# Two heads side by side in the rows of the matmul array, in the first attention of a four-layer model

## The reference, cut to what matters

```python
y = jnp.einsum('oc,bct->bto', W, x)            # Q, K, V: 16 heads of 16
att = jnp.einsum('bhqd,bhkd->bhqk', Q, K) * (1.0 / math.sqrt(Dh))
att = att + b[0]
m = mask[:, None, None, :]
att = att * m + (1.0 - m) * NEG_INF            # NEG_INF = -1e30
att = jax.nn.softmax(att, axis=-1)
y = jnp.einsum('bhqk,bhkd->bhqd', att, V)      # x = x + y, transposed back
```

## Time and profile before

| | us |
|---|---|
| median of 3 runs | 2042.97 (2039.57 to 2043.9) |
| the profiled execution's own time | 2042.31 |
| its span in the trace | 2040.5 |
| mean granted TensorE clock in it | 0.958 of full |
| both attentions with their preparations, to the end of the last scores stage | 0 to 1000 |
| second attention of the last item alone, recurrence, last layer | 1000 to 2040 |

### The profile page before, as it was taken

The page is one execution under the profiler, slowest core; times in us unless marked ns, Lnnn a source line. Parts: engine busy times, 40 slices in busy tenths (PEclk is TensorE's granted clock), DMA queues, the critical chain, the costliest instruction groups (busy, mean ns, idle before and its releaser), DMA issues. The chain is left out here.

```text
span 2040.5 us, 87545 instructions
## 1 busy us (share of the span) xinstructions
PE 1885.0 (92%) x33246; PEld 1408.9 (69%) x33246; DVE 1255.9 (62%) x5543; ACT 1095.2 (54%) x4105; POOL 380.2 (19%) x1398
## 2 busy tenths in 40 slices
PE   8887998999989999899887999999999999999996
PEld 4234454464644636446456999999999999999995
DVE  6545383654836447364333677777777777777767
ACT  0342736637356363654744466656666666666554
POOL 3000000000000000000000234343434333343335
PEclk7778999999999999999998999999999999999997
DMA  5122213223032230412223000000000000000002
GB/s 190 70 74 53 82 28 97 66 53 92 19 101 62 66 92 6 106 41 73 74 62 108 3 0 0 0 0 0 0 0 0 0 0 0 0 0 0 0 0 83
DMA packets 103527, 86.76 MB, mean 43 GB/s; under 512 B 15616, under 2 KB 90496, under 8 KB 103440
## 3 DMA queue, kind: packets, MB, share of 16 engines
q1 hardware_dynamic: 101392, 84.38, 14.4%
q10 hardware_dynamic: 1664, 1.18, 0.2%
q0 software_dynamic: 384, 0.01, 0.0%
HBM read 60.20 MB, written 21.00 MB: 40 GB/s over the span
## 5 line engine op out<-in xcount | busy, mean ns | idle before, releaser
L1255 PE MATMUL bank_pair_A<-moving,rep 128*128 128x16 f16 x8192 | 318.5, 170 | 2.5 <-ACT bank_pair_C L1346 1.4
L1255 PE MATMUL bank_pair_C<-moving,rep 128*128 128x16 f16 x8192 | 316.2, 169 | 0.0
L1255 PE MATMUL bank_pair_B<-moving,rep 128*128 128x16 f16 x8192 | 316.1, 169 | 0.0
L1255 PEld LDWEIGHTS bank_pair_A<-moving,rep 128*128 128x128 f16 x8192 | 274.7, 96 | 14.2 <-issue 4.0
L1355 ACT ACTIVATE r_gate<-r_pre 128x16 f32<-128x16 f32 x512 | 110.5, 216 | 286.5 <-DVE r_pre L1446 286.5
L1255 PEld LDWEIGHTS bank_pair_C<-moving,rep 128*128 128x128 f16 x8192 | 258.9, 96 | 0.0
L1255 PEld LDWEIGHTS bank_pair_B<-moving,rep 128*128 128x128 f16 x8192 | 258.9, 96 | 0.0
L1242 PE MATMUL bank_pair_D<-x_part,w_in 128*128 128x256 f16 x1536 | 198.6, 275 | 7.3 <-ACT gi_rz L1382 4.7
L1137 POOL TENSOR_TENSOR x<-x,w_in 128x512 f32<-128x512 f32 x8 | 10.2, 1272 | 960.5 <-DMA w_in<-w_in 960.5
L1446 DVE TENSOR_REDUCE r_pre<-bank_pair_A 128x16 f32<-128x32 f32 x512 | 98.1, 192 | 133.7 <-PE bank_pair_A L1255 133.7
L834 ACT ACTIVATE probs<-bank_pair_A 128x1024 f32<-128x1024 f32 x128 | 130.9, 1023 | 89.6 <-PE bank_pair_A L598 89.2
(11 more groups left out here) (262 smaller groups left out, 3786.0 us busy)
## 6 DMA issues: line engine op xcount, KB each, us to landing
rep<-parts SPq DMA_DIRECT2D x256, 64.0 KB
parts<-parts SPq DMA_DIRECT2D x48, 256.0 KB, 2.1
q_rep<-parts SPq DMA_DIRECT2D x32, 256.0 KB, 4.8
k_rep<-parts SPq DMA_DIRECT2D x64, 128.0 KB, 2.9
w_in<-in_x_dram SPq DMA_DIRECT2D x8, 512.0 KB, 4.0
x<-in_x_dram SPq DMA_DIRECT2D x8, 512.0 KB, 4.3
parts<-parts SPq DMA_DIRECT2D x32, 128.0 KB, 2.6
out_dram<-res SPq DMA_DIRECT2D x16, 256.0 KB, 2.0
```

The source lines that it names most:

```text
L1255: last = nc.tensor.matmul(ps[part][:, o:o + 2 * B], w[:, k, (first + c) * P:(first + c) * P + P], moving[j % 2][:, k, :, :].rearrange("p s ...
```

## The change

Two heads now stand in partitions 0 to 63 and 64 to 127 of `q_rep` and `k_rep`, and each matmul of the first attention has 64 rows; the two of a pair are issued one after the other, in different halves of the array's rows. The mask and bias partitions are gone: keys are centred by their masked mean (so that a masked key, now zero, has the score of the mean key), and mask and bias stand in the exponential's bias. The maximum is added by a second pair of matmuls of 64 rows. The functions keep their places in the order of steps.

```diff
             def load_rep(b, g):
...
-                sp.dma_start(k_rep[64:67, heads, :], mask_rows[b:b + 1, :, :].rearrange("o r t -> (o r) t").unsqueeze(1)
-                             .broadcast_to([3, 4, D])).then_inc(ld_rep[g], 16)
                 sp.wait_ge(st_parts, b * 64 + 64)
-                for rep0, rows in ((q_rep, ((0, 0), (0, 32), (1, 16), (1, 48))), (k_rep, ((2, 0), (2, 16), (3, 32), (3, 48)))):
-                    for n, row in rows:
-                        sp.dma_start(rep0[row:row + DH0, heads, :], parts0[n][heads, :, :].rearrange("h d t -> d h t")).then_inc(ld_rep[g], 16)
+                for s in range(2):
+                    heads, pairs = slice(4 * g + s, 4 * g + 4, 2), slice(2 * g, 2 * g + 2)
+                    for rep0, rows in ((q_rep, ((0, 0), (1, 16), (1, 32), (0, 48))), (k_rep, ((2, 0), (2, 16), (3, 32), (3, 48)))):
+                        for n, row in rows:
+                            row += s * P // 2
+                            sp.dma_start(rep0[row:row + DH0, pairs, :], parts0[n][heads, :, :].rearrange("h d t -> d h t")).then_inc(ld_rep[g], 16)
...
-                for qc in range(2):
-                    t0 = (2 * (u % 2) + qc) * P
-                    last = nc.tensor.matmul(pair[u % 2][:, qc, :], q_rep[0:96, u // 2, t0:t0 + P], k_rep[0:96, u // 2, :],
+                t0 = u % DC * P
+                for s, half in enumerate(HALF):
+                    last = nc.tensor.matmul(pair[u % 2][:, s, :], q_rep[half, u // DC, t0:t0 + P], k_rep[half, u // DC, :],
                                             start=True, stop=True)
...
-                for j in range(4):
-                    h = 4 * g + j
-                    last = nc.tensor.matmul(pair[u % 2][:, j // 2, (j % 2) * N:(j % 2) * N + N], k_rep[:, h, kc * P:kc * P + P],
-                                            q_rep[:, h, queries], start=(j % 2 == 0), stop=True, skip_group_check=True)
+                for s, half in enumerate(HALF):
+                    nc.tensor.matmul(pair[u % 2][:, s, :], k_rep[half, p, kc * P:kc * P + P], q_rep[half, p, :], start=True, stop=False)
+                for s, half in enumerate(HALF):
+                    last = nc.tensor.matmul(pair[u % 2][:, s, :], max_sel[half, :], max_rep[half, p, :], start=False, stop=True)
...
+                    nc.vector.scalar_tensor_tensor(out=kf[:, c, :], in0=k[:, c, :], scalar=1.0, in1=mask_bc[:, :], op0=ALU.mult,
+                                                   op1=ALU.mult, accum_out=key_sum[:, c:c + 1]).then_inc(k_sum, 1)
+                dve.wait_ge(k_sum, 3 * b + 2)
+                nc.vector.tensor_scalar(key_sum[:, :], key_sum[:, :], seen[:, 1, b:b + 1], None, ALU.mult).then_inc(k_sum, 1)
+                dve.wait_ge(k_sum, 3 * b + 3)
+                for c in range(NC):
+                    last = nc.vector.scalar_tensor_tensor(out=kf[:, c, :], in0=k[:, c, :], scalar=key_sum[:, c:c + 1], in1=mask_bc[:, :],
+                                                          op0=ALU.subtract, op1=ALU.mult)
```

More of the change, by code:

```diff
@@ L174, in attention @@
             cond_sb = mask_bc[0:B, :]
-            rows = y[0:B, :, :].rearrange("p a b -> p (a b)").bitcast(F16)[:, 0:3 * D].rearrange("p (r d) -> p r d", r=3)
             block = prep.enter_context(nc.Block())
@@ L250, in _ @@
                 last.then_inc(c_condt, 1)
+                pe.wait_ge(c_copied, 4)
+                for c in range(DC):
+                    last = nc.tensor.matmul(pC[:, 1, 0:B], ones32[:, 0:1].broadcast_to([P, P]), condT[:, c, :], start=(c == 0), stop=(c == DC - 1))
+                last.then_inc(c_count, 1)
         ld_x1, ld_mask, st_parts, ld_max = (sem(n) for n in ("ld_x1", "ld_mask", "st_parts", "ld_max"))
@@ L812, in k_part @@
                 act.wait_ge(kf_ok, b + 1)
-                nc.scalar.activation(k_hi[:, :, :], kf[:, :, :], ACT.Copy).then_inc(k_hi_ok, 1)
+                nc.scalar.activation(k_hi[:, :, :], kf[:, :, :], ACT.Copy, scale=QS).then_inc(k_hi_ok, 1)
             def v_part(b):
@@ L827, in max_rows @@
                 act.wait_ge(max_ok, b + 1)
-                act.dma_start(q_rep[96:97, :, :].rearrange("o h (c t) -> o (h c) t", c=DC), max_row[:, :]).then_inc(ld_max, 16)
+                for s in range(2):
+                    act.dma_start(max_rep[s * P // 2:s * P // 2 + 1, :, :].rearrange("o h (c t) -> o (h c) t", c=DC),
+                                  max_row[s * U0:s * U0 + U0, :]).then_inc(ld_max, 16)
             def exponent(b, u):
@@ L833, in exponent @@
                     act.wait_ge(pv_ps, b * W0 + (u // 2 - 1))
-                nc.scalar.activation(probs[u // 2 % 2][:, :, u % 2 * N:u % 2 * N + N],
-                                     pair[u % 2][:, :, :].rearrange("p a (b t) -> p (a b) t", b=2), ACT.Exp, scale=LOGIT0).then_inc(exp_ok, 1)
+                kc = u // 2 % DC
+                nc.scalar.activation(probs[u // 2 % 2][:, 2 * (u % 2):2 * (u % 2) + 2, :], pair[u % 2][:, :, :], ACT.Exp,
+                                     bias=mask_bias[:, kc, b:b + 1], scale=LOGIT0).then_inc(exp_ok, 1)
             def inverse(b, g):
@@ L977, in k_part @@
                 dve.wait_ge(k_hi_ok, b + 1)
-                nc.vector.tensor_tensor(k_lo[:, :, :], kf[:, :, :], k_hi[:, :, :], ALU.subtract).then_inc(k_lo_ok, 1)
+                nc.vector.scalar_tensor_tensor(out=k_lo[:, :, :], in0=kf[:, :, :], scalar=QS, in1=k_hi[:, :, :],
+                                               op0=ALU.mult, op1=ALU.subtract).then_inc(k_lo_ok, 1)
             def group_sums(b, g):
@@ L1120, in _ @@
         def _(pool):
-            pair_of_rows = float(np.array([ROW, ROW], np.float16).view(np.float32)[0])
             nc.gpsimd.memset(v_aug[:, :, :, DH0:], 1.0).then_inc(c_later, 1)
```

86 lines of the change are left out of this document (38 added, 48 removed).

## The result

| | median us (lowest to highest) | ratio to the kernel before, 95% interval |
|---|---|---|
| before | 2041.96 (2039.57 to 2043.90) | |
| changed | 2081.61 (2080.13 to 2082.90) | 1.0188 (1.0174 to 1.0202) |

The change makes the kernel 39.6 us slower; 15 were predicted. The span of the profiled execution grew from 2040.5 to 2078.0. I cut it at the first attention's exponentials: a scores stage reaches from the start of an item's first to the end of its last, a maxima stage from there to the next item's first. Both columns of the table are differences to the kernel before.

What follows compares the result with a forecast made beforehand. PE, busy 92% of the span, was taken as the bound. Scores stages +22.2, maxima stages -15.6 and start +8.3 gave +14.9 on 2042.3, that is 2057, forecast as 2058 us for the median; range 2028 to 2088 (80%).

Steps and rivals of the forecast that it cites:

- a pair costs 0.22 (512 columns) plus 0.007: First attention's matmuls: two in different row halves overlap as strips do, taking 0.22 us plus 0.007; without overlap 0.43.
- Price 0.097 at full clock: PE, each switch between full-array matmuls and matmuls of 64 rows: 0.097 us, as for strips; the other end is 0.
- 12 + 7 = 19 changes, 1.84 us: Scores stage: twelve q, k, v projection slots each add a mode change before, seven also one behind; 1.84 us, unhidden.
- The 0.41 for DVE: Second attention's maxima, eight slots: PE waits 0.41 us within each pair, hiding all but one mode change, leaving 0.4 us.
- 2.54 a stage: Scores stage of items 1 to 6, without the centred-key wait: units 0.2, mode changes 1.84, 0.4 and 0.1 us.
- The exponential keeps its shape, its bias costs nothing: First attention's exponential on ACT: same shape as before, and the added bias operand takes no time.
- Centred keys, 0.7: Scores stages of items 1 to 6: PE waits 0.7 us for `kf`, delayed by two more passes and one small step.
- Maxima stages: Half-row units shorten the stage by 2.1 us an item, six times -12.6; item 0 -3 (0 to -6); sum -15.6.
- Groups between `weigh1`: Maxima stage, four units between two `weigh1`, paced by DVE: -0.33 us a group, three groups -1.0.
- the gain of 3 that was predicted: Item 0's maxima stage, units in threes and part of it at half clock: -3 us (0 to -6).
- Start: Before the first exponential: later bias load +4.9, centred keys +1.6, 16 DMA issues +2.6, among others; +8.3 us.
- weights load in the open: Rival: the pair's second matmul starts one load (0.10 us) late, adding 25 to 50 us, 2080 to 2105; chance 11%.

## Why the prediction was wrong

The direction was right, and most of the working on mode and overlap too. The size failed, by 22.6 us of span: 10.2 in the scores stages, 8.0 in the maxima stages of items 1 to 6 and 5.9 in item 0's, less 0.9 at the start and 0.6 at the end. Two steps failed with their cause shown: the price of a change of mode left out the weight load behind it, and the exponential's bias was put at nothing. Item 0's maxima stage is a third, and its cause stays open.

- **"a pair costs 0.22 (512 columns) plus 0.007", "Price 0.097 at full clock": right.** The halves overlap, and a change costs 0.09 to 0.10. That strips of 32 and 8-row transposes speak for 64 rows, and 96 rows do not, held. The Trainium skill (TensorEngine Tiling (Array Packing), Key Properties) has a change of mode drain the engine, and these 0.09 to 0.10 agree with it. The load in the open comes on top.
- **Changes in the scores stage, "12 + 7 = 19 changes, 1.84 us": mis-sized.** The mechanism was right, the price of one was not: a slot behind a change pays for 0.10 of weight load too, and so each of the twelve slots costs that much more than I charged. With units and boundaries I had 2.54 a stage; 3.0 were measured, not 2.54 + 1.2. I take the rest to fall where PE waits anyway, which no run isolates. The 0.41 for DVE in this sum was also misread, as said above.
- **"The exponential keeps its shape, its bias costs nothing": this step failed.** It costs 0.09 each, 23 us of ACT time, of which 0.45 us a stage reached the end in items 1 to 6, and 1.3 in item 7, because a pair without slots now takes ACT as long as PE. That makes 5 us in all. Two rows of before gave the price, and I had not looked at them.
- **Centred keys, 0.7: 0.9 at full clock**, with 0.78 shown as PE's wait. The second pair of passes took 1.41 where 1.29 was reckoned, and the reads of the sums 0.08 each.
- **Maxima stages: mis-sized twice.** Groups between `weigh1` gave what was predicted; among f32 work the same weight load in the open took most of the rest (nine times 0.10), so 1.0 a stage came in place of 2.1. That is 6.6 of the 8.0 us; the other 1.4 is clock, which was below 1.00 in four of the six stages here and in three of six before. In item 0 the stage grew by 2.9 against -3. PE had less to do there than before (53.92 against 57.50 us busy), but more of it at half clock: 0.76 against 0.79 granted, and 0.81 with maxima of all rows, whose stage was 79.7 with 55.90 busy. Over all profiled executions the stage took 80.6 to 85.2 with halves and 79.7 to 82.6 without, so the gain of 3 that was predicted never appeared. Why the clock fell differently was not isolated.
- **Start: +7.4 for +8.3, by other parts, and partly by luck.** PE's first projection came at 14.27 (15.5 predicted), since the bias landed at 13.2; from there to the first load it took 2.8 more than before (1.6 predicted); the issues cost 2.1 (2.6); the first reduction was due near 41 and came at 41.6. But the kernel before had its quickest start in the execution that was profiled. With the same start, the kernel with the operand added reached its first exponential at 79.5 and those with another order at 79.6 and 78.0, because the 64 matmuls behind the projections (L780) took 11.1 there for 8.7, at a granted clock of 0.63 for 0.81. There the first reduction came 9.3 to 9.5 after the first load was issued, and in the changed kernel 9.4. Against these three the change costs 3 to 6 us at the start, and none of it between those two points.
- The rival "weights load in the open" had the second half's weights in mind, which are hidden. Its mechanism was wrong. The time fell into its range of 2080 to 2105 by luck: another load in the open gave 8 to 10 us of the miss, the operand 5 and item 0's maxima stage 6.

## What to carry to other kernels

Group matmuls that are packed by halves of rows. Each one that stands alone between full f32 matmuls costs two changes of mode and one weight load, 0.29 us here, which is more than the 0.21 it saves. Grouping saves PE's time, but it shortens a stage only if nothing else, here DVE's reductions, sets the pace of the group. Before calling an added operand free, look in the same trace for two instructions of one engine and shape that differ in it. When a change multiplies DMAs, count the issues on the queue at the one place where nothing covers them. And compare parts of one profiled execution with several others that share the same code there: here the start of the kernel before varied by 4 us.

## What the runs showed of the hardware that was not expected

- The first f32 matmul behind a change of mode shows 0.10 us of weight load: eight matmuls of L644 took 1.99 for 1.89, a slot of L553 1.12 for 1.02, and in the kernel before eight matmuls of L640 2.00 for 1.89 behind transposes of 64 columns.
- A per-partition bias operand adds 0.09 us to an activation at both shapes that the runs have (474 against 383 ns at 128 x 256, 1112 against 1023 at 128 x 1024).
- Loading the same bytes from two queues cut the time from the first issue to the first reduction from 9.43 to 5.97 us.
- Less work on PE did not always mean less time: item 0's maxima stage, with 3.6 us less PE work, was 2.9 longer at a lower granted clock.
